# Two layers of a four-layer image network: the first layer's normalisation with pixels on the partitions, and the second layer's patch transform ahead of its input convolution

## The chip, the core and the metric

The kernel runs on one NeuronCore of a Trainium2 chip. The metric is the device time of one execution in microseconds (us), all data already in the chip's memory. PE is the matrix engine, PEld its weight loads, DVE the vector engine, ACT the scalar engine, POOL the engine that here issues gathers, SP the queue that issues the other transfers.

## The reference, cut to what matters

The input is 4 images of 48 channels of 256 x 256 pixels in f32. Four layers follow each other, each with a group normalisation ahead and a residual sum behind. The change touches the first two.

```
first layer:   qkv = depthwise3x3(conv1x1(x))            # q, k, v of 96 channels each
               out = irfft2(rfft2(q_patch) * rfft2(k_patch))   # 8 x 8 patches
               normed = (out - mean_c(out)) / sqrt(var_c(out) + 1e-5) * gamma + beta
               y = conv1x1(v * normed)
second layer:  y = w_in @ x                              # 48 -> 288 channels
               y = irfft2(rfft2(y_patch) * fft_mask)     # 8 x 8 patches, mask by channel
               y = depthwise3x3(y);  y = w_out @ (gelu(y1) * y2)
```

The mean and the variance of the first layer are over the 96 channels of one pixel. In the second layer `w_in` mixes channels and the patch transform mixes pixels, so that either may be done first. The third layer reads boxes of an integral image at computed places; the fourth is like the second.

## The kernel before, in words

`build` runs per image: first layer (`layer0`), second layer (`layer1`), integral image, front of the third layer. The boxes of the third layer are gathers (`Boxes`, POOL), their arithmetic is on DVE and their transposes on PE. They run inside other layers: image b's boxes, half of them, inside the first layer of image b + 1, the other half inside its second layer. So image 0 has both layers without boxes, and images 1 to 3 have them with boxes. The last image's boxes run inside the fourth layer.

Every engine has its own instruction list, written out by hand in program order; semaphores tie them together (`wait_ge`, `then_inc`). Nothing reorders the work.

**First layer.** A strip is 8 rows; an image has 32 strips, a strip has four steps of 512 pixels: 128 steps per image, 512 in all. `pipeline` (L407) unrolls eight steps in a loop body. In a step `n` PE does, in this order: the q and k convolutions of the first half (`conv_qk`, L516 and L519, pixels on the output's partitions); the output convolution of step n - 2 (L552); with boxes, at every other step, the transposes of one box unit (`boxes.turn`, L1803); for step n - 1 the inverse transform (L563, channels on the partitions); the second half of `conv_qk`; for step n - 1 the mean's removal as a product with a 96 x 96 matrix (L575), the v convolution (`conv_pass`, L285 and L289), and the variance (L584, one column per 128 pixels); the forward transforms of step n (L533); and for step n - 1 the spread of 1/sqrt over the channels' partitions (L592). ACT evacuates: `conv` L617, squares L628, root L631, `rb` L642, gamma and beta L645, copies of q and k L610 and of the spectra L638, and the split of the operands into two parts (L298). DVE has the reciprocal L707, the spectral products L714, the normalised value L719, its product with v L724, the residual sum L688 with statistics L692, the other half of the split L303, and with boxes the `blend` of one unit at odd steps (L1760 to L1777).

**Second layer.** A strip of 8 rows has 16 tiles of 128 pixels; 33 strips per image pass (`pipeline`, L804, two strips in a loop body). At slot t of a strip PE does the input convolution of tile t (L975, 49 rows deep, 304 columns), the forward transform of tile t - 1 (L918), the inverse of tile t - 2 (L925, three products of 128 columns), taps of the depthwise convolution of the strip before (L943, in small tiles of the array side by side), and at some slots the output convolution (L996 to L1002) and a box unit's transposes (L1803). ACT copies between the first two products (L1043), DVE multiplies by the mask (L1100) and does the rest of the depthwise convolution as a chain (L1111, L1114), the products with the gelu, the residual and, with boxes, the box arithmetic.

**Boxes.** POOL issues 16 gathers per unit. Each waits for a count (`paced`) that PE raises 16 times per unit, and may run ahead of it by `lead`. There are two buffers for gathered data (`used` frees one).

## Time and profile before

| what | us |
|---|---|
| median of the runs | 25524.35 |
| lowest and highest of 3 | 25506.17, 25534.23 |
| the profiled execution, and its span | 25507.03, 25505.5 |
| PE busy in the span | 23815.7 (93%) |
| DVE, POOL, ACT busy | 15811.9, 10957.5, 7039.7 |
| mean granted clock of PE | 0.951 |

Busy times of PE are ends as modelled of pipelined products, so a span that is full of them may still be spent on few columns. A slot of PE's time is better read from the start of one group to the start of the next. "PEclk" is the granted share of full clock; 1.00 is 2.4 GHz, a half is 1.2 GHz. In a window's row each number in brackets is a count of instructions.

### The profile page before, as it was taken

To read this page: it belongs to the slowest core of one execution; us is meant where nothing else is said; L and a number is where in the kernel's file an instruction comes from. 1 tells how busy PE (TensorE), PEld (TensorE's weight loads), DVE (VectorE), ACT (ScalarE), POOL (GpSimd) and SP (SyncE) were. 2 spreads that over 40 slices of the span, in tenths; PEclk is the share of its full clock that TensorE was granted. 3 is DMA by queue.
4 is the path that set the end of the run, shared out by engine and by line. 5 is a ranking of instruction groups with operands and counts; after the bars stand their busy time and mean duration, and the time that the engine had idled before them with its cause. 6 is when DMAs were issued, how large, how long until landed. Compare 5 with 4: busy or idle time off the path is not lost. (4 is left out here: it accounts for less than half of the span.)

```text
span 25505.5 us, 440196 instructions
## 1 busy us (share of the span) xinstructions
PE 23815.7 (93%) x147480; PEld 16191.6 (63%) x147480; DVE 15811.9 (62%) x23975; ACT 7039.7 (28%) x13096; POOL 10957.5 (43%) x8564
## 2 busy tenths in 40 slices
PE   6998998989999999899999988999999889998999
PEld 5775555667765556577655565777555647676767
DVE  4445555556668874566688845665888556666643
ACT  2333332123333321233333301333333112222222
POOL 0000000046656640366566602665666118787820
PEclk9999998899999998999999979999999799999999
DMA  3220001444432224444322234443222246666643
GB/s 81 57 62 26 20 21 43 115 100 102 99 76 80 79 69 110 105 102 100 80 80 78 75 94 111 101 102 84 79 79 80 82 116 136 136 142 133 140 92 73
DMA packets 875645, 2256.60 MB, mean 88 GB/s; under 512 B 257480, under 2 KB 509132, under 8 KB 762800
## 3 DMA queue, kind: packets, MB, share of 16 engines
q1 hardware_dynamic: 454512, 1309.67, 22.8%
q0 software_dynamic: 419840, 928.94, 14.4%
q8 instruction: 902, 14.78, 0.2%
q14 instruction: 391, 3.20, 0.0%
HBM read 1860.59 MB, written 385.13 MB: 88 GB/s over the span
## 5 line engine op out<-in xcount | busy, mean ns | idle before, releaser
L1706 POOL DMA_INDIRECT e_got<-table,e_idx x6144 | 7892.7, 1285 | 4230.8 <-issue 1766.9
L1722 POOL DMA_INDIRECT e_got<-table,e_idx x2048 | 2776.9, 1356 | 706.8 <-issue 492.6
L1114 DVE SCALAR_TENSOR_TENSOR b_acc<-b_z,b_dwc,b_acc 112x1024 f32<-112x1024 f32 x2112 | 2617.4, 1276 | 4.2
L285 PE MATMUL d_p<-d_xs,d_ws 125*96 125x512 f32 x9216 | 2480.7, 414 | 80.8 <-issue 57.2
L516 PE MATMUL a_p_qk<-a_wst,a_stack 125*128 125x192 f32 x12288 | 2424.1, 333 | 26.1 <-DMA a_stack<-in_xp 8.4
L1043 ACT ACTIVATE b_ys<-b_p_in 128x304 f32<-128x304 f32 x2112 | 893.8, 423 | 5223.8 <-PE b_p_in L975 5223.7
L943 PE MATMUL b_p_conv<-b_z,b_diag_a 64*64 64x512 f32 x19008 | 2277.7, 599 | 1.5 <-DVE b_g_a L1129 1.5
L1760 DVE TENSOR_TENSOR e_got<-e_got,e_wt 128x1536 f32<-128x1536 f32 x1024 | 1772.5, 1747 | 693.2 <-DMA e_got<-table,e_idx 690.2
L1100 DVE TENSOR_TENSOR b_ym<-b_p_f,b_mask 128x304 f32<-128x304 f32 x2112 | 1001.3, 474 | 1796.3 <-PE b_p_f L918 1785.8
L516 PEld LDWEIGHTS a_p_qk<-a_wst,a_stack 125*128 125x128 f32 x12288 | 2012.1, 190 | 123.8 <-ACT a_qh L638 80.2
L925 PEld LDWEIGHTS b_p_z<-const,b_ym 128*66 128x66 f32 (+2 forms) x12672 | 1649.3, 171 | 429.4 <-issue 32.9
L285 PEld LDWEIGHTS d_p<-d_xs,d_ws 125*96 125x96 f32 x9216 | 1479.5, 166 | 665.2 <-issue 84.8
L925 PE MATMUL b_p_z<-const,b_ym 128*66 128x128 f32 (+2 forms) x12672 | 1773.2, 276 | 13.0 <-ACT b_z L1031 12.8
L975 PE MATMUL b_p_in<-b_w,b_xt 66*128 66x304 f32 x4224 | 1632.2, 469 | 161.7 <-issue 157.4
L1233 POOL DMA_DIRECT2D i_x<-planes x128 | 66.3, 518 | 3796.9 <-issue 2339.0
L975 PEld LDWEIGHTS b_p_in<-b_w,b_xt 66*128 66x128 f32 x4224 | 674.2, 195 | 1502.8 <-issue 1489.6
L918 PE MATMUL b_p_f<-b_ys,const 128*128 128x304 f32 x4224 | 1466.5, 428 | 5.3 <-DVE b_ym L1100 5.3
L310 PE MATMUL c_p_g<-c_stack,c_wst 125*96 125x512 f32 x3072 | 1430.3, 602 | 26.0 <-issue 26.0
L1766 DVE TENSOR_TENSOR e_got<-e_got 128x1536 f32<-128x1536 f32 (+1 forms) x1024 | 1387.1, 1355 | 24.2
L285 PE MATMUL a_p_v<-a_xs,a_ws 125*96 125x512 f32 x4608 | 1371.4, 442 | 0.0
L707 DVE RECIPROCAL a_rs<-a_sd 128x4 f32<-128x4 f32 x512 | 89.6, 175 | 1962.3 <-ACT a_sd L631 1962.3
L943 PEld LDWEIGHTS b_p_conv<-b_z,b_diag_a 64*64 64x64 f32 x19008 | 625.8, 132 | 873.9 <-issue 750.9
(274 smaller groups left out, 40024.3 us busy)
## 6 DMA issues: line engine op xcount, KB each, us to landing
e_got<-table,e_idx POOLq DMA_INDIRECT x8192
a_stack<-in_xp SPq DMA_DIRECT2D x256, 387.0 KB
c_stack<-planes SPq DMA_DIRECT2D x256, 387.0 KB
d_stack<-planes SPq DMA_DIRECT2D x256, 387.0 KB
table<-i_acc SPq DMA_DIRECT2D x256, 384.0 KB, 2.3
b_x<-planes SPq DMA_DIRECT2D x132, 395.1 KB
b_xr<-planes SPq DMA_DIRECT2D x264, 197.5 KB
planes<-b_out SPq DMA_DIRECT2D x264, 197.5 KB
```

What stands on the lines that cost most here:

```text
L285: mm = pe.matmul(out, ws[i][:, dx, lo:hi], xs[j][:, r0:r0 + QROWS, dx:dx + W], start=(dx == i == j == 0), stop=False)
L310: pe.matmul(out, wst[:, dx, lo:hi], stack[:, r0:r0 + QROWS, dx:dx + W], start=(dx == 0), stop=False)
L516: m = pe.matmul(dst_, st[:, row, dx + 128 * t:dx + 128 * t + 128], wst[:, dx, 0:2 * C2], start=(dx == 0), stop=False)
L918: pe.matmul(p_f[:, 0:NC], env.c("dft"), ys[k % 2][:], start=True, stop=True).then_inc(f_ready, 1)
L925: mm = pe.matmul(p_z[g][0:MZ[g], k % 4 * 128:k % 4 * 128 + 128], ym[k % 2][:, LO[g]:LO[g] + MZ[g]], env.c("idft"), start=True, stop=True)
L943: mm = pe.matmul(p_conv[r][size * c:size * (c + 1), :], diag[size * r:size * (r + 1), k, :], zs[g][size * r:size * (r + 1), QROWS * q + dy ...
L975: pe.matmul(p_in[:, 0:NC], xt[par][:, t, :], w[:], start=True, stop=True).then_inc(in_ready, 1)
L1114: dve.scalar_tensor_tensor(out=a, in0=rows, scalar=dwc[0:M[D], D, k:k + 1], in1=a, op0=ALU.mult, op1=ALU.add).then_inc(chain, 1)
L1706: pool.indirect_dma_start(out=self.got[q][:, t, c * REC:(c + 1) * REC], out_offset=None, in_=self.flat, in_offset=bass.IndirectOffsetOnAxi ...
L1722: pool.indirect_dma_start(out=self.got[q][:, t, c * REC:(c + 1) * REC], out_offset=None, in_=self.flat, in_offset=bass.IndirectOffsetOnAxi ...
L1760: dve.tensor_tensor(part, part, self.wt[i][:, at:at + 32].unsqueeze(2).broadcast_to([128, 32, C]), ALU.mult).then_inc(self.halved, 1)
L1766: dve.tensor_tensor(got[:, :, 0:half], got[:, :, 0:half], got[:, :, half:2 * half], ALU.add).then_inc(self.halved, 1)
```

## The change

First layer: the inverse transform is done as two products with the transform as stationary operand, one per half of the pixels, into partitions 0 to 63 and 64 to 127 (`p_o`, 384 columns: 4 tiles of 96 channels). Pixels now lie on the partitions, so the sum over channels is along the row. ACT takes the sum and the sum of squares with an accumulating output (`accum_out`, four instructions each, one per 96 columns), the root, and the normalised value with a scale and a bias per pixel (four instructions); DVE adds `shift`. PE then transposes `nrm` back (four products with the identity, into `p_c`), and ACT applies gamma and beta (`gain`). The 96 x 96 product, the variance's four products and the spread of 1/sqrt are gone. The output convolution of step n - 2 stands behind the second half of `conv_qk`. On DVE the product with v opens the step, the spectral products close it, and a box unit's blend is spread over two steps. POOL's lead goes from 16 to 20.

Second layer: two neighbouring tiles of 49 input planes are taken together on 113 partitions (a second transfer loads the planes shifted by 16 pixels). PE turns them to pixels (`turned`, 128 columns), transforms them (`spectrum`, 128 columns), and then convolves each tile's spectrum to 304 columns (`widen`, two products from partitions 0 to 63 and 64 to 127, into two banks). ACT copies between them. The multiplication by the mask is done for two tiles at even slots, with four buffers instead of two.

The diff, cut to its core and moved left:

```diff
-        boxes.gather(pool, 0, U, 16)
+        boxes.gather(pool, 0, U, 20)
...
-        if back2:
-            pe.wait_ge(t3_ready, n - 1)
-            pe.wait_ge(sd_ready, n - 1)
-            pe.wait_ge(res_ready, n - 2)
-            pe.matmul(p_y[0:WIDE, :], wo[:], t3[k % 2][:], start=True, stop=True).then_inc(y_ready, 1)
...
-            pe.wait_ge(t1_ready, n - 1)
+            pe.wait_ge(gain_ready, n - 1)
             boxes.turn(pe, *turned(u, k), p_c)
...
-            pe.wait_ge(rb_ready, n - 1)
-            for t in range(4):
-                for h in range(2):
-                    m = pe.matmul(p_o[0:C2, t * 128 + h * 64:t * 128 + h * 64 + 64], prod[(k - 1) % 2][:, h, t, :],
-                                  env.c("combine"), start=True, stop=True)
-                    if beat and t == h == 0:
-                        boxes.beat(m)
+            pe.wait_ge(nrm_ready, n - 1)
+            for h in range(2):
+                m = pe.matmul(p_o[64 * h:64 * h + 64, 0:4 * C2], env.c("combine"),
+                              prod[(k - 1) % 2][:, h, :, :], start=True, stop=True)
+                if beat and h == 0:
+                    boxes.beat(m)
             m.then_inc(o_ready, 1)
         if front:
             conv_qk(k, n, 1)
+        if back2:
+            pe.wait_ge(t3_ready, n - 1)
+            pe.wait_ge(res_ready, n - 2)
+            pe.matmul(p_y[0:WIDE, :], wo[:], t3[k % 2][:], start=True, stop=True).then_inc(y_ready, 1)
         if back:
-            pe.wait_ge(o_copied, n)
-            pe.wait_ge(t1_ready, n - 1)
-            if boxes and turn_box:
-                boxes.bank_free(pe, *turned(u, k))
-            pe.matmul(p_c[0:C2, :], env.c("center"), conv[:], start=True, stop=True).then_inc(c_ready, 1)
...
             conv_pass(pe, p_v[0:C2, :], ws, we, xs[(k - 1) % 2], xe[(k - 1) % 2], 0, 0, C2,
                       boxes.beat if beat else None, (1, 8)).then_inc(v_ready, 1)
...
-            pe.wait_ge(sq_ready, n)
-            pe.wait_ge(res_ready, n - 1)
-            for t in range(4):
-                m = pe.matmul(p_y[:, t:t + 1], sq[:, 128 * t:128 * t + 128], env.c("mean96"), start=True, stop=True)
-            m.then_inc(var_ready, 1)
         if front:
             transforms(n, k)
...
-            pe.wait_ge(rs_ready, n)
+            pe.wait_ge(nrm_ready, n)
+            pe.wait_ge(gain_ready, n - 1)
+            if boxes and turn_box:
+                boxes.bank_free(pe, *turned(u, k))
             for t in range(4):
-                m = pe.matmul(p_o[0:C2, 128 * t:128 * t + 128], rs[:, t:t + 1].broadcast_to([128, C2]), env.c("ident"), start=True, stop=True)
+                m = pe.matmul(p_c[0:C2, 128 * t:128 * t + 128], nrm[:, t, :], env.c("ident"), start=True, stop=True)
...
+        if back2:
+            act.wait_ge(turned_ready, n - 1)
+            act.wait_ge(t3_ready, n - 2)
+            act.activation(gain[:], p_c[0:C2, :], ACT.Identity, bias=beta[:], scale=gamma[:]).then_inc(gain_ready, 1)
...
         if back:
             act.wait_ge(o_ready, n)
-            act.wait_ge(c_ready, n - 1)
-            act.activation(conv[:], p_o[0:C2, :], ACT.Copy).then_inc(o_copied, 1)
+            act.wait_ge(nrm_ready, n - 1)
+            for t in range(4):
+                s = act.activation(junk[:, t, :], p_o[:, C2 * t:C2 * t + C2], ACT.Copy, accum_out=total[:, t:t + 1])
+            s.then_inc(total_ready, 1)
+            act.wait_ge(total_ready, n)
+            act.wait_ge(shift_ready, n - 1)
+            act.activation(mu[:], total[:], ACT.Copy, scale=-1.0 / C2).then_inc(mu_ready, 1)
+            act.wait_ge(mu_ready, n)
+            for t in range(4):
+                s = act.activation(junk[:, t, :], p_o[:, C2 * t:C2 * t + C2], ACT.Square, bias=mu[:, t:t + 1],
+                                   accum_out=square[:, t:t + 1])
+            s.then_inc(sq_ready, 1)
         if front:
             copy_qk(1)
+        if back:
+            act.wait_ge(sq_ready, n)
+            act.wait_ge(rs_ready, n - 1)
+            act.activation(sd[:], square[:], ACT.Sqrt, bias=env.eps[:, 0:1], scale=1.0 / C2).then_inc(sd_ready, 1)
...
-            act.wait_ge(c_ready, n)
-            act.wait_ge(var_ready, n - 1)
-            act.activation(sq[:], p_c[0:C2, :], ACT.Square).then_inc(sq_ready, 1)
-            act.wait_ge(var_ready, n)
-            act.wait_ge(rs_ready, n - 1)
-            act.activation(sd[:], p_y[:, 0:4], ACT.Sqrt, bias=env.eps[:, 0:1]).then_inc(sd_ready, 1)
+            act.wait_ge(shift_ready, n)
+            act.wait_ge(turned_ready, n - 1)
+            for t in range(4):
+                s = act.activation(nrm[:, t, :], p_o[:, C2 * t:C2 * t + C2], ACT.Identity,
+                                   bias=shift[:, t:t + 1], scale=rs[:, t:t + 1])
+            s.then_inc(nrm_ready, 1)
...
-        if back:
-            act.wait_ge(b_ready, n)
-            act.wait_ge(t1_ready, n - 1)
-            act.activation(rb[:], p_o[0:C2, :], ACT.Copy).then_inc(rb_ready, 1)
-            act.wait_ge(t1_ready, n)
-            act.wait_ge(t3_ready, n - 1)
-            act.activation(t1[:], t1[:], ACT.Identity, bias=beta[:], scale=gamma[:]).then_inc(t2_ready, 1)
...
         if back2:
-            kk = (k - 2) % 8
-            r0 = QROWS * (kk % 4)
-            rows = out[kk // 4][:, r0:r0 + QROWS, 1:1 + W]
-            dve.wait_ge(y_ready, n - 1)
-            if kk % 4 == 0:
...
-            dve.scalar_tensor_tensor(out=rows, in0=p_y[0:CP, :].rearrange("p (y x) -> p y x", x=W), scalar=bo[:, 0:1],
-                                     in1=rows, op0=ALU.add, op1=ALU.add).then_inc(res_ready, 1)
...
-        if boxes and turn_box:
-            boxes.residual(dve, *turned(u, k), p_c)
+            dve.wait_ge(gain_ready, n - 1)
+            dve.wait_ge(v_ready, n - 1)
+            dve.wait_ge(y_ready, n - 3)
+            dve.tensor_tensor(t3[k % 2][:], p_v[0:C2, :], gain[:], ALU.mult).then_inc(t3_ready, 1)
...
-        if boxes and front and k % 2:
-            boxes.blend(dve, u, k // 4, k // 2 % 2)
+        if boxes and front:
+            for part in ((1, 2) if k % 2 else (0,)):
+                boxes.part(dve, u, k // 4, k // 2 % 2, part)
+        if boxes and turn_box:
+            boxes.residual(dve, *turned(u, k), p_c)
+        if back2:
+            kk = (k - 2) % 8
+            r0 = QROWS * (kk % 4)
+            rows = out[kk // 4][:, r0:r0 + QROWS, 1:1 + W]
+            dve.wait_ge(y_ready, n - 1)
+            if kk % 4 == 0:
...
+            dve.scalar_tensor_tensor(out=rows, in0=p_y[0:CP, :].rearrange("p (y x) -> p y x", x=W), scalar=bo[:, 0:1],
+                                     in1=rows, op0=ALU.add, op1=ALU.add).then_inc(res_ready, 1)
         if back:
             dve.wait_ge(sd_ready, n)
-            dve.wait_ge(b_ready, n - 1)
+            dve.wait_ge(nrm_ready, n - 1)
             dve.reciprocal(rs[:], sd[:]).then_inc(rs_ready, 1)
...
-            dve.wait_ge(y_ready, n - 2)
-            dve.tensor_tensor(t3[(k - 1) % 2][:], p_v[0:C2, :], t1[:], ALU.mult).then_inc(t3_ready, 1)
+            dve.wait_ge(rs_ready, n)
+            dve.tensor_tensor(shift[:], mu[:], rs[:], ALU.mult).then_inc(shift_ready, 1)
+        if back2:
+            dve.wait_ge(res_ready, n - 1)
+            q = n - n_first - 2
...
+            for h in range(2):
+                bank = p_f[1] if h == 0 else p_qk[1]
+                dve.wait_ge(qh_copied, 2 * n + h + 1)
...
+                dve.tensor_tensor(prod[k % 2][:, h, :, :].rearrange("p t c -> p (t c)"), bank[0:NPROD, 0:4 * C2],
+                                  qh[:, h, :, :].rearrange("p t c -> p (t c)"), ALU.mult).then_inc(prod_ready, 1)
...
-xt = [sb(f"xt{i}", [WIDE, NT, 128]) for i in range(2)]
-x, xr, out = sb("x", [CP, SROWS, WP]), sb("xr", [128, 2, QROWS, WP]), sb("out", [128, 2, QROWS, WP])
...
+xt = [sb(f"xt{i}", [128, NH, 128]) for i in range(2)]
+xp = [sb(f"xp{i}", [128, 128]) for i in range(2)]
+xf = [sb(f"xf{i}", [128, 128]) for i in range(2)]
...
-ym = [sb(f"ym{i}", [128, NC]) for i in range(2)]
+ym = [sb(f"ym{i}", [128, NC]) for i in range(4)]
...
-p_in, p_f, p_y = pb("p_in"), pb("p_f"), pb("p_y")
+p_in, p_y = [pb("p_in0"), pb("p_in1")], pb("p_y")
...
+        sp.dma_start(x[0:CP, :, :], planes(src, b, 0, CP, s * SROWS + 1, SROWS)).then_inc(x_loaded, 16)
+        sp.dma_start(x[64:PAIR, :, :], shifted(src, b, 0, CP, s * SROWS + 1, 16)).then_inc(x_loaded, 16)
...
+    def turned(n, i, k):
+        if k == 0:
+            pe.wait_ge(xt_ready, n + 1)
+        pe.wait_ge(masked, n * NT + 2 * (k - 1))
+        pe.wait_ge(t_copied, n * NH + k)
+        pe.matmul(p_in[0][:, FROM:FROM + 128], xt[i][:, k, :], env.c("ident"), start=True, stop=True).then_inc(t_ready, 1)
     def spectrum(n, k):
-        pe.wait_ge(in_copied, n * NT + (k + 1))
-        pe.wait_ge(masked, n * NT + k)
-        pe.matmul(p_f[:, 0:NC], env.c("dft"), ys[k % 2][:], start=True, stop=True).then_inc(f_ready, 1)
+        pe.wait_ge(t_copied, n * NH + (k + 1))
+        pe.wait_ge(masked, n * NT + 2 * k)
+        pe.wait_ge(f_copied, n * NH + k)
+        pe.matmul(p_in[1][:, FROM:FROM + 128], xp[k % 2][:], env.c("dft"), start=True, stop=True).then_inc(f_ready, 1)
+    def widen(n, k, more):
+        pe.wait_ge(t_copied, n * NH + (k + 2 if more or k + 2 < NH else NH))
+        pe.wait_ge(f_copied, n * NH + (k + 1))
+        pe.wait_ge(masked, n * NT + 2 * k)
+        for h in range(2):
+            pe.matmul(p_in[h][:, 0:NC], xf[k % 2][64 * h:64 * h + 64, :], w[64 * h:64 * h + 64, :],
+                      start=True, stop=True).then_inc(in_ready, 1)
...
-            if front:
-                if t == 0:
-                    pe.wait_ge(xt_ready, n + 1)
-                pe.wait_ge(in_copied, n * NT + t)
-                pe.matmul(p_in[:, 0:NC], xt[par][:, t, :], w[:], start=True, stop=True).then_inc(in_ready, 1)
-            if front and t >= 1:
-                spectrum(n, t - 1)
-            if mid and t == 0:
-                spectrum(m, NT - 1)
+            if front and t % 2 == 0:
+                widen(n, t // 2, more)
...
+            if front and t % 2:
+                if t + 3 < NT:
+                    turned(n, par, t // 2 + 2)
+                elif more:
+                    turned(n + 1, 1 - par, (t - 13) // 2)
+                if t + 1 < NT:
+                    spectrum(n, t // 2 + 1)
+                elif more:
+                    spectrum(n + 1, 0)
...
-        act.activation(xt[i][0:CP].rearrange("p t (y x) -> p t y x", x=16),
-                       x[:, :, 1:1 + W].rearrange("p y (t x) -> p t y x", x=16), ACT.Copy).then_inc(xt_ready, 1)
+        act.wait_ge(x_loaded, (n - 1) * 32)
+        act.wait_ge(t_ready, (n - 1) * NH)
+        act.activation(xt[i][0:PAIR].rearrange("p t (y x) -> p t y x", x=16),
+                       x[:, :, 1:1 + W].rearrange("p y (t g x) -> p t g y x", g=2, x=16)[:, :, 0], ACT.Copy).then_inc(xt_ready, 1)
+    def copy_turned(n, k):
+        act.wait_ge(t_ready, n * NH + (k + 1))
+        act.wait_ge(f_ready, n * NH + (k - 1))
+        act.activation(xp[k % 2][:], p_in[0][:, FROM:FROM + 128], ACT.Copy).then_inc(t_copied, 1)
+    def copy_spectrum(n, k):
+        act.wait_ge(f_ready, n * NH + (k + 1))
+        act.wait_ge(in_ready, n * NT + 2 * (k - 1))
+        act.activation(xf[k % 2][:], p_in[1][:, FROM:FROM + 128], ACT.Copy).then_inc(f_copied, 1)
...
-            if front:
-                act.wait_ge(in_ready, n * NT + (t + 1))
-                act.wait_ge(f_ready, n * NT + (t - 1))
-                act.activation(ys[t % 2][:], p_in[:, 0:NC], ACT.Copy).then_inc(in_copied, 1)
+            if front and t % 2:
+                if t + 3 < NT or more:
+                    copy_turned(n + (t + 3) // NT, (t // 2 + 2) % NH)
+                if t + 1 < NT or more:
+                    copy_spectrum(n + (t + 1) // NT, (t // 2 + 1) % NH)
...
     def weigh(n, k):
-        dve.wait_ge(f_ready, n * NT + (k + 1))
-        dve.wait_ge(inv_ready, n * NT + (k - 1))
-        dve.tensor_tensor(ym[k % 2][:], p_f[:, 0:NC], mask[:], ALU.mult).then_inc(masked, 1)
+        dve.wait_ge(in_ready, n * NT + (k + 1))
+        dve.wait_ge(inv_ready, n * NT + (k - 3))
+        dve.tensor_tensor(ym[k % 4][:], p_in[k % 2][:, 0:NC], mask[:], ALU.mult).then_inc(masked, 1)
...
-                weigh(n, t - 1)
-            if mid and t == 0:
-                weigh(m, NT - 1)
+            if front and t % 2 == 0:
+                weigh(n, t)
+                weigh(n, t + 1)
```

## Rows read from the trace of the kernel before

**Rows 1.** The page, part 1: busy us, share of the span, instructions.

```profile
PE 23815.7 (93%) x147480; PEld 16191.6 (63%) x147480; DVE 15811.9 (62%) x23975; ACT 7039.7 (28%) x13096; POOL 10957.5 (43%) x8564
```

**Rows 2.** Windows: stretch and length, busy us (instructions) by engine, PEclk, DMA, GB/s.

```profile
1003.49:1123.60 120.11, 119.00 (x704) 92.66 (x704) 55.58 (x97) 44.95 (x89) 0.00 (x0) 1.00 0.27 60
6009.76:6133.32 123.56, 122.41 (x736) 96.06 (x736) 75.40 (x109) 45.02 (x89) 80.33 (x65) 1.00 0.45 100
3082.50:3208.10 125.60, 123.22 (x928) 65.33 (x928) 73.46 (x98) 40.72 (x74) 0.00 (x0) 0.97 0.07 21
8139.20:8269.40 130.20, 125.79 (x961) 68.20 (x961) 107.39 (x134) 40.75 (x74) 85.00 (x64) 0.97 0.29 79
```

**Rows 3.** Timeline of PE, one step of the first layer: start, us, line, count.

```profile
1003.49 1.07 PE L552 MATMUL a_p_y<-a_t,a_wo 96*66 96x512 f32 x2
...
1004.40 1.50 PE L563 MATMUL a_p_o<-const,a_prod 94*96 94x64 f32 x16
...
1005.74 1.19 PE L516 MATMUL a_p_qk<-a_wst,a_stack 125*128 125x192 f32 x6
...
1008.40 1.02 PE L575 MATMUL a_p_c<-a_conv,const 96*96 96x512 f32 x2
...
1012.04 0.95 PE L584 MATMUL a_p_y<-const,a_sq 96*128 96x1 f32 x8
...
1012.93 0.56 PE L533 MATMUL a_p_f<-a_qk,const 64*94 64x384 f32 x1
...
1013.32 0.48 PE L533 MATMUL a_p_f<-a_qk,const 64*94 64x384 f32 x1
...
1013.65 0.48 PE L533 MATMUL a_p_f<-a_qk,const 64*94 64x384 f32 x1
...
1014.39 1.11 PE L592 MATMUL a_p_o<-const,a_rs 128*96 128x128 f32 x8
...
1015.48 1.24 PE L516 MATMUL a_p_qk<-a_wst,a_stack 125*128 125x192 f32 x6
...
1018.48 0.65 PE L552 MATMUL a_p_y<-a_t,a_wo 96*66 96x512 f32 x1
```

**Rows 4.** Groups by line and shape, second layer, two strips with boxes.

```profile
L1002 PE MATMUL b_p_y<-b_g_d,b_wo 112*64 112x512 f32 x16 | 4.3, 618 | 0.0
```

**Rows 5.** Groups by line and shape, whole span, ACT.

```profile
L645 ACT ACTIVATE a_t<-a_t,a_beta,a_gamma 96x512 f32<-96x512 f32 x512 | 416.0, 812 | 386.8 <-DVE a_t L719 386.8
...
L617 ACT ACTIVATE a_conv<-a_p_o 96x512 f32<-96x512 f32 x512 | 303.6, 593 | 1225.5 <-PE a_p_o L563 1225.5
...
L631 ACT ACTIVATE a_sd<-a_p_y,eps 128x4 f32<-128x4 f32 x512 | 134.7, 263 | 1248.8 <-PE a_p_y L584 1248.8
```

**Rows 6.** Timeline of DVE in the first layer with boxes.

```profile
6028.23 3.40 DVE L1760 TENSOR_TENSOR e_got<-e_got,e_wt 128x1536 f32<-128x1536 f32 x2
```

**Rows 7.** Timeline of PE in the second layer, around the head of the loop.

```profile
8130.03 0.68 PE L975 MATMUL b_p_in<-b_w,b_xt 66*128 66x304 f32 x2
...
8130.55 0.68 PE L918 MATMUL b_p_f<-b_ys,const 128*128 128x304 f32 x2
...
8131.06 0.82 PE L925 MATMUL b_p_z<-const,b_ym 128*66 128x128 f32 x6
...
8131.81 2.81 PE L943 MATMUL b_p_conv<-b_z,b_diag_e 32*32 32x512 f32 x48
...
8139.17 1.38 PE L975 MATMUL b_p_in<-b_w,b_xt 66*128 66x304 f32 x2 [4.56 <-issue]
...
8140.34 1.22 PE L918 MATMUL b_p_f<-b_ys,const 128*128 128x304 f32 x2
```

**Rows 8.** Groups of POOL, eight steps of the first layer with boxes.

```profile
L1706 POOL DMA_INDIRECT e_got<-table,e_idx x65 | 82.3, 1266 | 43.6 <-issue 15.0 <-PE a_p_qk L519 11.2 <-PE a_p_f L533 7.3
```

**Rows 9.** Windows again: the integral image after the second layer, and the fourth layer.

```profile
4300.00:4640.00 340.00, 300.87 (x1764) 297.25 (x1763) 156.26 (x562) 28.43 (x58) 14.34 (x28) 0.68 0.32 101
21500.00:23900.00 2400.00, 2197.86 (x11623) 1665.60 (x11624) 1496.74 (x2024) 530.01 (x930) 1926.00 (x1419) 0.96 0.66 138
```

108 lines of the change are left out of this document (55 added, 53 removed).

## The prediction

> **What bounds the kernel now.** I read the page's busy times first [rows 1]: PE is busy 93% of the span, DVE 62%, POOL 43%, ACT 28%. An average over layers says little, so I then took windows of whole periods [rows 2]: eight steps of the first layer without and with boxes (120.11 and 123.56 us), and two strips of the second layer from loop head to loop head, without and with boxes (125.60 and 130.20 us). The reader is to see that PE is busy for all but 1 us in the first layer's two windows and that no other engine comes near; in the second layer PE is idle for 2.4 and 4.4 us, and DVE, with boxes, has 107.39 of 130.20 us filled. So both layers go at PE's pace now, and DVE is the next limit in the second layer with boxes. Last I read PE's timeline by starts [rows 3, 7]: what a group costs is the time from its start to the next group's.
>
> **First layer, the slots of one step** [rows 3]: output convolution 0.91 us (1003.49 to 1004.40), inverse transform 1.34, second half of q and k 2.66, mean and v convolution together 3.64, variance 0.89, forward transforms 1.46, spread of 1/sqrt 1.09, first half of q and k with the wait behind it 3.00. Sum 14.99.
>
> Removed: the variance, 0.89. The mean's product, two passes of 512 columns as the output convolution has: 0.91 less about 0.03 for the change of shape, 0.88. The wait of 0.13 (my reading of 3.00 less 2.66, the rest being the change of shape) at the output convolution goes too: PE waits there for `t3`, and the output convolution now stands 3.4 us later, behind the inverse transform and the second half of q and k. Where the step then waits next is weighed below.
>
> Changed: the inverse transform has 16 passes of 64 columns and gets four of 384 columns, two by two in the array's two column halves. That form is in the trace in the second layer's output convolution [rows 4]: 16 passes of 512 columns keep PE busy for 4.3 us, 1.08 per four, though two passes of 512 one after the other cost 0.88. So the halves run side by side. The forward transforms show two passes of 384 columns per 0.33 us (1013.32 to 1013.65) [rows 3], so I take 2 x 0.33 + 0.09 for the switch = 0.75. Bounds: 0.65, and 1.40 if the halves run one after the other. Gain taken 0.59. The spread's eight passes of 128 columns become eight passes of 128 columns of transposes: no change.
>
> Sum: 0.89 + 0.88 + 0.13 + 0.59 = 2.49 us per step, a step of 12.50. The trace has 128 steps without boxes and 384 with; with boxes the turn of a unit adds (123.56 - 120.11)/4 = 0.86 every second step, unchanged, so 15.44 becomes 12.95. Gains: 128 x 2.49 = 319 us and 384 x 2.49 = 956 us.
>
> What could stand in PE's way is the chain from the inverse transform to the transposes: ACT's four sums, the negated mean, four squares, a copy of q and k, the root, two splits; DVE's reciprocal and shift; ACT's four normalisations. Between the two PE has 2.66 + 0.91 + 2.76 + 1.46 = 7.8 us of other work. The prices: an ACT operation over 512 columns takes 593 ns with no pointer, 812 with scale and bias as pointers, one over 4 columns with one pointer 263 [rows 5]. By the slope from 4 to 512 columns I estimate 96 columns at 0.26 us, 0.34 with a bias, 0.44 with both. No row shows an accumulating output: between nothing and a whole further small operation, 0.26, each. I take 0.1, since the four sums read no more than the one copy (L617) that they replace. Then the squares end 4 x 0.26 + 0.2 + 4 x 0.34 + 0.8 = 3.4 us after the inverse transform, the root at about 4.2, the splits at 5.3; DVE's reciprocal stands behind the residual sum, which waits for the output convolution (3.6 us, plus 0.3 of latency, plus 0.74), so at about 4.9, shift 5.2; the normalisations end at 7.0. That is 0.8 us inside the cover. With the accumulation at 0.26 they end at 7.6 to 7.8: still just inside. ACT's total rises from 45 us per eight steps [rows 2] to some 65 of 100.
>
> DVE with boxes: 75.40 us per eight steps [rows 2], less one product of 0.6 and plus a shift of 0.2 per step, some 72 of 103.6. The two weighings of a unit take 3.40 us [rows 6] and now stand ahead of the residual sum at even steps. From the end of `t3` (1 us before the inverse transform ends, at most) they end 2.4 us behind it, the box residual 1.4 later, at 3.8, and the sum is due at 3.9. This is tight but covered, if the gathers have landed.
>
> Gathers: 16 per two steps. At present each takes 1.27 us of POOL plus 0.30 of issue [rows 8], 25 us per unit; two steps will last 25.9. So POOL goes from half idle to nearly full and a late gather will hold DVE, hence PE, now and then. The unit is also weighed a step earlier, and the lead of four more makes good half a step of that. Between nothing and the fourth layer's rate (1419 gathers in 2400 us, 1.69 each, 27.0 per unit [rows 9], 0.55 per step over mine, 211 us) I take 50 us. The second layer's extra transfer falls where the DMA share is 0.07 to 0.29 [rows 2]; I price it at nothing.
>
> **Second layer, two tiles** [rows 7]: convolution 0.52 and transform 0.51 each, 2.06 for two tiles; the inverse 0.75 for six passes of 128 columns stays. Added: four passes of 128 columns at 0.125, 0.50; and the widened pair, four passes of 304 columns from two row halves. The first layer's forward transforms are such pairs and run side by side [rows 3], so 2 x 0.25 + 0.05 = 0.55. Bounds 0.50 and 1.05. Gain 2.06 - 1.05 = 1.01 per two tiles, 8.1 per strip. Without boxes DVE has 73.46 us of work in 125.60 [rows 2] and stays under PE's: 33 strips x 8.1 = 267 us.
>
> With boxes DVE is the limit. Its 107.39 us of busy time per two strips and about 0.04 us for each of its 134 instructions (my estimate of the pauses between dependent ones) give 112.8. PE would need 123.6 - 16.2 = 107.4 between the loop's heads. The head costs more: PE idles 4.56 us at it and then runs its first products at half clock, 1.17 us against 0.52 [rows 7], some 6.8 us in all on top of 2 x 61.6. PE can't be far ahead of DVE there: `turned` at odd slots waits for both mask products of the slot before, on DVE. I take the head's 6.8 us as added to DVE's time, 119.6 per two strips against 130.20; the bounds are 113 (hidden wholly) and 123. Gain 5.3 per strip, 99 strips: 525 us; 500 with the first strips of each image, which have no full load.
>
> Starts of the four images cost some 10 us (a serial chain turned, copied, transformed, copied; a memset ahead of the first load).
>
> **Sum**: 319 + 956 - 50 + 267 + 500 - 10 = 1982 us off the profiled execution's 25,507, so 23,525. That execution lay 17 us under the median of three; the median of the changed kernel I put at 23,540.
>
> **Rivals.**
> 1. POOL sets the pace of the first layer with boxes, at the fourth layer's rate: 161 us more, 23,700. For it: 25 of 25.9 us is nearly no slack, and gathers of over 4 us hide in that mean of 1.27. Against it: the fourth layer's DMA share is 0.66, this one's would be 0.54.
> 2. The second layer's loop head is hidden under DVE's backlog: 113 per two strips, 8.6 per strip, 850 in place of 500 less the load of the first strips, 23,250. Against it stands the wait of `turned`.
> 3. ACT's small operations are late: an accumulation at 0.5 us each puts eight of them 3.2 us behind my 0.8 and beyond the cover by some 2.4 us; 512 steps x 2.4 = 1230, 24,770; half of that, 24,150, at 0.35. For it: no row has such an instruction.
> 4. The halves don't run side by side in these new forms: 0.65 x 512 = 333, and 0.5 x 8 x 33 = 132, and about 130 in the strips with boxes: 24,135. Against it are rows 3 and 4.
> 5. The other side: in the second layer with boxes PE waits for DVE at every odd slot, and the clock falls as at the loop head and stays at half. At present it falls after a gap of 4.56 us [rows 7], and where PE's work is broken by waits for long, the window's mean is 0.68 [rows 9]. PE's 53.5 us per strip would be about 105, 40 over today's 65.1, x 99 = 3960; with the gains of the first layer and of image 0 (1482) the time is 27,985. It decides once some 37% of these strips' time is at half. Against it: the waits that I see are about 1 us, between stretches of taps, and the first layer has such short waits at a clock of 1.00 [rows 2].
>
> On this rival the Trainium skill, page "TensorE: Matmul & The Clock Gate", section "HAM oscillation — how this bites in real kernels", says that a loop in which each burst of matmuls is followed by a wait pays the return to the half rate on every turn. By that rule, and only if my 1 us were long enough, the kernel would be the slower one; the loop head in rows 7 does just what the rule says, and no row shows it for waits of 1 us.
>
> **How the numbers follow.** Forecast 47%, rival 1 17%, rival 2 12%, rival 3 14%, rival 4 6%, rival 5 4%. The range of 80% reaches from 23,200 (below rival 2) to 24,250 (over rivals 1 and 4 and the half of rival 3). A measurement of this kernel tells 0.2%, about 50 us, from no change. Only rival 5 or a far worse rival 3 ends slower: faster 0.95, same 0.01, slower 0.04.
>
> **What would show it.** Eight steps of the first layer should take 100 us without boxes and 103.6 with; the inverse transform's slot 0.75; PE's wait ahead of the transposes under 0.2 us. In the second layer two strips take 109 us without boxes and 120 with, where DVE's idle time is at the loop head only. I am wrong if ACT's accumulating operations take over 0.5 us, if PE waits for `nrm` or for `f_copied` in every step, or if the granted clock in the second layer with boxes is under 0.9.

## The result, and the profile after

The changed kernel takes 23,558.65 us (median of 4; 23,545.67 to 23,576.81), against 25,515.26 for the kernel before: ratio 0.9233, interval 0.9217 to 0.9249. The forecast was 23,540. Its profiled execution has a span of 23,544.1 us at a mean granted clock of 0.945.

The page of the changed kernel, part 1, against [rows 1]:

```profile
PE 21720.1 (92%) x136216; PEld 14130.0 (60%) x136216; DVE 15356.9 (65%) x23979; ACT 7710.4 (33%) x22312; POOL 10986.6 (47%) x8568
```

TensorE (PE) lost 2,096 us of work and stays the engine that is busy all the time. ScalarE (ACT) has only 671 us more work, but 9,216 more instructions.

Windows of the changed kernel, with the columns of [rows 2]: eight steps of the first layer without and with boxes, then two strips of the second without and with boxes.

```profile
1134.64:1239.23 104.59, 102.33 (x530) 73.17 (x528) 51.26 (x98) 63.24 (x236) 0.00 (x0) 0.98 0.31 70
5223.66:5334.42 110.76, 105.70 (x562) 77.40 (x561) 70.41 (x108) 62.91 (x234) 88.57 (x66) 0.98 0.52 113
3036.63:3146.55 109.92, 107.31 (x928) 52.72 (x929) 71.98 (x98) 33.64 (x74) 0.00 (x0) 0.97 0.10 31
7748.69:7862.77 114.08, 110.34 (x961) 55.45 (x961) 105.08 (x134) 33.67 (x74) 78.41 (x64) 0.98 0.36 98
```

The forecast for the four was 100, 103.6, 109 and 120. The first two are longer, and PE is now idle for 2.3 and 5.1 us in them where it was idle for 1 us before; the third is close to the forecast (109.0 in the mean of image 0's loop turns), the fourth 6 us shorter.

PE's timeline of one undisturbed step of the first layer, which answers to [rows 3]:

```profile
1058.94 1.02 PE L568 MATMUL a_p_y<-a_t,a_wo 96*66 96x512 f32 x2
1059.40 2.66 PE L285 MATMUL a_p_v<-a_xs,a_ws 125*96 125x512 f32 x9
...
1062.69 0.56 PE L534 MATMUL a_p_f<-a_qk,const 64*94 64x384 f32 x1
...
1064.16 1.11 PE L583 MATMUL a_p_c<-const,a_nrm 128*96 128x128 f32 x8
1065.25 1.24 PE L517 MATMUL a_p_qk<-a_wst,a_stack 125*128 125x192 f32 x6
...
1068.05 0.87 PE L557 MATMUL a_p_o<-a_prod,const 94*64 94x384 f32 x4
1068.85 1.24 PE L517 MATMUL a_p_qk<-a_wst,a_stack 125*128 125x192 f32 x6
...
1071.56 0.59 PE L568 MATMUL a_p_y<-a_t,a_wo 96*66 96x512 f32 x1
```

From start to start it is 12.62 us: output and v convolution 3.75, forward transforms 1.47, transposes 1.09, q and k with the combine pass between them 2.80 + 0.80 + 2.71. The combine slot (L557) tells that the column halves run side by side: 0.80 us for four passes of 384 columns.

PE around the second layer's loop head, against [rows 7]:

```profile
7742.83 2.81 PE L971 MATMUL b_p_conv<-b_z,b_diag_e 32*32 32x512 f32 x48
7748.69 0.94 PE L945 MATMUL b_p_in<-b_w,b_xf 64*128 64x304 f32 x4 [3.05 <-issue]
7749.56 1.55 PE L953 MATMUL b_p_z<-const,b_ym 128*66 128x128 f32 x6
```

Where the 1,961 us between the two spans lie, by stretches of the two traces (the first layer from its first to its last q/k product, the second from there to the integral image):

| stretch | forecast gain | measured |
|---|---|---|
| first layer, image 0 | 319 | 257 (1,918 to 1,661) |
| first layer, images 1 to 3 | 906 | 745 (1,989 to 1,741 each) |
| second layer, image 0 | 267 | 258 |
| second layer, images 1 to 3 | 500 | 718 |
| starts; fourth layer, whose code is the same | -10; 0 | within the rows above; -21 (4,535 to 4,557) |

The total is right by luck: the first layer gives 223 us less than forecast and the second 209 us more. What the experiments had to find is each of these errors. Some 43 us of the second layer's two rows are the passage to it, from the last q/k product to its own first product, which is 9 to 12 us shorter in each image (80 to 70 in image 0, about 71 to 60 in the others). Experiment 1 shows that most of this comes with the first layer's change.

ACT's groups of the changed kernel over the whole span, which take the place of [rows 5]:

```profile
L639 ACT ACTIVATE a_nrm<-a_p_o,a_shift,a_rs 128x96 f32<-128x96 f32 x2048 | 715.1, 430 | 268.1 <-DVE a_shift L716 263.9 <-issue 4.2
L620 ACT ACTIVATE a_junk<-a_p_o,a_mu 128x96 f32<-128x96 f32 x2048 | 669.4, 339 | 16.6
...
L613 ACT ACTIVATE a_junk<-a_p_o 128x96 f32<-128x96 f32 x2048 | 482.5, 250 | 426.7 <-PE a_p_o L557 426.7
L613 ACT ACTIVATION_READ_ACCUMULATOR a_junk<-a_p_o 128x1 f32 x2048 | 423.5, 207 | 0.0
```

An accumulating output is an instruction of its own, 0.207 us long, though the next one starts 0.09 us after it (1148.47 and 1148.56 us in one step). The estimates of 0.26, 0.34 and 0.44 us for 96 columns hold: 0.25, 0.34, 0.43.

Two kinds of stall are new. In image 0, PE's waits (engine, line, what it waited for; us, times, longest):

```profile
PE a_p_f L534 <- ACT a_qk L601: 27.7, 13, 2.9
PE a_p_c L583 <- ACT a_nrm L639: 5.8, 8, 0.9
```

Thirteen times, once for each turn of the loop. ACT's own waits there name nothing on which it depends:

```profile
ACT a_qk L601 <- issue: 53.5, 13, 4.5
ACT a_gain L606 <- issue: 50.4, 13, 4.8
```

ACT stands still for about 3.9 us at the jump back (before L606) and 4.1 in the middle of the body (before L601), while everything it needs is ready. In images 1 and 2 there are no such gaps, and image 3 has the 13 at the jump alone. The trace also records the jump instruction itself (L408): from it to the next instruction that ACT's sequencer takes up there are 4.4 us in image 0 and 4.6 in image 3 (medians), and 0.24 in images 1 and 2, which run the same code. So the sequencer itself stands still there.

In image 1 (4850 to 6450 us) PE waits for something else:

```profile
PE a_p_c L583 <- ACT a_nrm L639: 37.2, 21, 5.0
```

and VectorE's (DVE) timeline at one of these times says why:

```profile
5228.30 1.76 DVE L1803 TENSOR_TENSOR e_got<-e_got,e_wt 128x1536 f32<-128x1536 f32 x1 [8.44 <-DMA e_got<-table,e_idx]
...
5232.08 0.16 DVE L714 RECIPROCAL a_rs<-a_sd 128x4 f32<-128x4 f32 x1
5232.27 0.16 DVE L716 TENSOR_TENSOR a_shift<-a_mu,a_rs 128x4 f32<-128x4 f32 x1
```

The weights wait 8.44 us for gathered records; reciprocal and shift stand behind them in DVE's order, `nrm` behind shift, and PE's transposes behind `nrm`, 4.99 us. From 5216 to 5231 the DMA engines are busy without a break (1.04), with SyncE's loads of the next strip (`a_stack`, `a_rest`, `a_out`, the box unit's weights) among the gathers. And the wait costs more than itself. Three windows:

```profile
5216.00:5231.00 15.00, 12.93 (x71) 9.32 (x69) 5.91 (x7) 6.04 (x25) 11.83 (x11) 1.00 1.04 178
5229.00:5233.00 4.00, 0.00 (x0) 0.00 (x0) 3.80 (x7) 0.53 (x2) 3.39 (x3) 1.00 0.95 230
5233.90:5238.00 4.10, 4.08 (x19) 4.08 (x20) 2.51 (x5) 1.48 (x3) 2.16 (x2) 0.62 0.31 87
```

After 5 us without work PE runs at a granted clock of 0.62 over 4.1 us, that is for most of it at 1.2 GHz in place of 2.4. This step takes 18.90 us, 6.28 over the ordinary.

### The profile page after: what moved, and what is told of

Read it like the earlier page. It is cut to its first block and busy times, and to the rows that moved or that the text cites. A ratio compares the mean times of both kernels' runs of the same rounds, so it can differ in the third digit from the quotient of the medians.

```text
span 23544.1 us, 427591 instructions
## 1 busy us (share of the span) xinstructions
PE 21720.1 (92%) x136216; PEld 14130.0 (60%) x136216; DVE 15356.9 (65%) x23979; ACT 7710.4 (33%) x22312; POOL 10986.6 (47%) x8568
## 5 line engine op out<-in xcount | busy, mean ns | idle before, releaser
L1803 DVE TENSOR_TENSOR e_got<-e_got,e_wt 128x1536 f32<-128x1536 f32 x1024 | 1781.8, 1751 | 1038.5 <-DMA e_got<-table,e_idx 1035.5
L953 PEld LDWEIGHTS b_p_z<-const,b_ym 128*66 128x66 f32 (+2 forms) x12672 | 1513.9, 172 | 1104.6 <-issue 888.1
L953 PE MATMUL b_p_z<-const,b_ym 128*66 128x128 f32 (+2 forms) x12672 | 1860.0, 286 | 15.3 <-ACT b_z L1070 15.3
L1056 ACT ACTIVATE b_xp<-b_p_in 128x128 f32<-128x128 f32 x1056 | 292.7, 277 | 4699.9 <-PE b_p_in L932 4689.7
L1144 DVE TENSOR_TENSOR b_ym<-b_p_in,b_mask 128x304 f32<-128x304 f32 x2112 | 899.5, 468 | 779.4 <-PE b_p_in L945 775.1
L971 PE MATMUL b_p_conv<-b_z,b_diag_e 32*32 32x512 f32 x19008 | 1118.8, 596 | 2.1 <-DVE b_g_a L1172 2.1
L285 PEld LDWEIGHTS a_p_v<-a_xs,a_ws 125*96 125x96 f32 x4608 | 747.9, 162 | 540.2 <-issue 284.9
L709 DVE SCALAR_TENSOR_TENSOR a_out<-a_p_y,a_bo,a_out 49x512 f32<-49x512 f32 x512 | 379.5, 741 | 1038.7 <-PE a_p_y L568 1038.2
L520 PE MATMUL a_p_qk<-a_wrs,a_rest 66*128 66x192 f32 x4096 | 1010.9, 327 | 0.0
```

The lines of the kernel that those rows point to most:

```text
L285: mm = pe.matmul(out, ws[i][:, dx, lo:hi], xs[j][:, r0:r0 + QROWS, dx:dx + W], start=(dx == i == j == 0), stop=False)
L520: m = pe.matmul(dst_, rt[:, row, 128 * t:128 * t + 128], wrs[:, 0:2 * C2], start=False, stop=True)
L953: mm = pe.matmul(p_z[g][0:MZ[g], k % 4 * 128:k % 4 * 128 + 128], ym[k % 4][:, LO[g]:LO[g] + MZ[g]], env.c("idft"), start=True, stop=True)
L971: mm = pe.matmul(p_conv[r][size * c:size * (c + 1), :], diag[size * r:size * (r + 1), k, :], zs[g][size * r:size * (r + 1), QROWS * q + dy ...
L1144: dve.tensor_tensor(ym[k % 4][:], p_in[k % 2][:, 0:NC], mask[:], ALU.mult).then_inc(masked, 1)
L1803: dve.tensor_tensor(part, part, self.wt[i][:, at:at + 32].unsqueeze(2).broadcast_to([128, 32, C]), ALU.mult).then_inc(self.halved, 1)
```

## The experiments

Twelve kernels. "The changed kernel" is 23,558.65 us throughout. Totals of kernels timed on different chips can differ by some 10 to 20 us, and the integral image's stretch, the same code in all, goes from 360 to 417 us between traces; so the stretches of the traces are compared, not the totals alone.

**1. Each layer's change alone.** The old function `layer1` beside the new `layer0`, and the other way round.

```
first_only:   layer0 of after, layer1 of before
second_only:  layer0 of before, layer1 of after
```

> The first layer as changed, the second as it was before. The terms of the forecast ask for 319 us in image 0 and 906 us in images 1 to 3: 25,515 - 1,225 = 24,290 us. Theory from the two traces: the first layer's stretch in the changed kernel became shorter by 257 us in image 0 and by 745 us in images 1 to 3, and nothing of the second layer's gain depends on it, so 25,515 - 1,001 = 24,515 us (24,480 to 24,550). Rival: part of the changed kernel's gain exists only with both layers changed (the transfers and gathers of one run under the other), and the time is over 24,560 us.

> The first layer as before, the second as changed. The terms of the forecast ask for 267 + 500 - 10 = 757 us: 24,758 us. Theory from the two traces: the second layer's stretch became shorter by 258 us in image 0 and by 718 us in images 1 to 3: 25,515 - 976 = 24,540 us (24,500 to 24,580). If the two sum to the whole change, this ratio and the other's gains add up to 1,957 us. Rival: the second layer's gain beyond the forecast came with the changed first layer, and alone it gives 757 us.

Measured: 24,546.7 us, ratio 0.9616 (0.9600 to 0.9632), as expected, and 24,605.2 us, 0.9639 (0.9623 to 0.9655), 25 us beyond the range. In the traces the new first layer gives 248, 251, 243 and 221 us in images 0 to 3, as against 257, 246, 250 and 249 with both changed. The new second layer gives 244, 232, 233 and 222 us within its own products (from the first that turns or convolves a tile to the last inverse), as against 250, 225, 227 and 236 with both changed. The shorter passage between the two layers, 43 us over the four images, comes with the first layer's change (44 us with it alone, 9 with the second alone). The expectation for `second_only` had counted it with the second layer, which is most of what it missed. So each layer keeps its own gain, and the error of the forecast is in each layer, not in how they meet.

The single gains add up to 977 + 919 = 1,896 of 1,957 us. Of the missing 61, 21 are the fourth layer's, whose time is 4,557 and 4,562 us here, as with the whole change: either change costs them, so the sum of the two counts them twice. Another 38 are the first layers, which gain less when alone: ScalarE's gaps are then in images 0, 1 and 3, not in 0 and 3, and image 3, with 26 gaps, is 27 us longer than with both.

**2. ScalarE without the sums** (mean and variance are left out; ones stand in for them).

```
-  s = act.activation(junk[:, t, :], p_o[...], ACT.Copy, accum_out=total[:, t:t + 1])
+  s = act.activation(junk[:, t, :], p_o[...], ACT.Copy)
   (the squares likewise; DVE fills total and square with ones once)
```

> The changed kernel without the accumulated outputs of the first layer's copies and squares (the sums that give mean and variance are left out; two tiles filled with ones stand in for them). That takes 8 instructions of 0.20 us a step out of ScalarE's list. Theory A (ScalarE's list is too long to be fetched in time: gaps of 3 to 5 us at the loop's head and in the body's middle, which hold the whole step): the gaps go, one step in eight of image 0 falls from 15 to 18.7 us to 12.6, which gives about 27.7 + 5.8 us per 320 us, some 130 us over image 0 and 27 us or more in image 3; sum 100 to 200 us faster, 23,360 to 23,460 us. Rival B (the gaps come from something else in the loop, say its own branch and address arithmetic, or transfers): they stay, and the time moves by less than 30 us. Rival C: ScalarE's busy time itself is what holds PE: then every step, not one in eight, becomes shorter.

Measured: 23,503.85 us, 0.9213 (0.9198 to 0.9229). The gaps are gone in all images (26 and 13 before, now 0), and image 0's first layer is 1,617 us in place of 1,661. A step without a stall stays at 12.61: rival C is out. The mechanism of theory A is there, and my size for it was wrong by three: the 27.7 + 5.8 us were those of the whole image, which I had taken for those of 320 us. Image 3, which was to gain 27 us or more, gains nothing: its first layer takes 1,745 us, 1,740 before, though its 13 gaps are gone; experiment 3 shows what takes their place. Eight instructions less a step cure the gaps, but this changes length and place at once.

**3. Only the place.** 48 increments of a semaphore ahead of ScalarE's list in each image.

```
   act.wait_ge(weights_loaded, 16 * NLOAD * (b + 1))
+  for _ in range(48):
+      act.sem_inc(turn, 1)
```

> The changed kernel with 48 semaphore increments (a few tens of ns each) ahead of ScalarE's list in the first layer of every image: the loop's body is the same and as long, and only its place in the list moves, by 48, 96, 144 and 192 instructions in images 0 to 3. Theory P (each of the 13 gaps of an image is a fetch whose moment is set by where the body lies in the list): the images and places with gaps change (now image 0 at the jump back and in the middle, image 3 at the jump back, images 1 and 2 none), and the time moves by 10 to 60 us either way. Rival Q (the gaps depend on the body's length and on what else runs in that image, the others' loads in image 0 or the four gather buffers in image 3): the same images show the same 26, 0, 0 and 13 gaps, and the time is the same within 15 us.

Measured: 23,537.57 us, 0.9218 (0.9204 to 0.9232). The total tells little, the trace more: neither of the two gaps in any image (ScalarE's jump takes 0.24 us in all four), and eight steps of image 0 take 100.98 us, with PE busy for all but 0.07:

```profile
1112.13:1213.11 100.98, 100.91 (x531) 72.34 (x529) 50.59 (x96) 63.16 (x234) 0.00 (x0) 1.00 0.32 72
```

Image 0's first layer is 1,619 us, as without the sums. The body is the same, as long as before, and next to the same loads: rival Q falls. The best reading of the 3.9 us is then a wait for instructions whose moment depends on where the body lies. The traces show no engine waiting for instructions by name; "issue" at the same two places, thirteen times, that goes when the list is moved, is how far they reach.

What a gap costs is another matter. Image 3's first layer stays as long without its gaps, 1,746 us for 1,740. PE's waits there, changed kernel and this one:

```profile
PE a_p_c L1846 <- ACT a_gain L606: 27.1, 13, 2.3
```

```profile
PE a_p_c L583 <- ACT a_nrm L641: 41.7, 19, 5.9
```

The second kind of stall, that of the late gathers, comes up where the first has gone. So the gaps by themselves are worth 42 to 44 us in image 0 and nothing in image 3.

**4. Shorter list by other means.** The same mean and variance by another formula: one square over 384 columns on ScalarE; two sums, the square of the total and the variance on DVE.

```
-  4 copies and 4 squares with accum_out, mu
+  act.activation(junk, p_o[:, 0:4 * C2], ACT.Square)
+  dve.reduce_sum(total[:], p_o as (t c), axis=X);  dve.reduce_sum(square[:], junk[:], axis=X)
+  both = total * total;  var = square * -96 + both
```

> The changed kernel with the same result by a shorter list for ScalarE: one square over all 384 columns in place of 4 squares, 4 copies, their 8 accumulator reads and the mean, and on VectorE two sums over 96 channels for the 4 columns, the square of the total and the variance (E[x2] - mean2). ScalarE issues 16 instructions less a step, VectorE 4 more, about 1.4 us a step, where it is idle 4.6 us a step in images 1 to 3. Theory (the 3.9 us gaps after the jump back and in the body come from the length of ScalarE's list): image 0's first layer falls from 1,661 to about 1,617 us, as without the sums, image 3's by 10 to 30 us; 23,470 to 23,520 us if VectorE's additions stay hidden. Rival: the sums come after the box unit's part on VectorE, so shift and normalised pixels are late in the steps with boxes; at 0.5 us a step over 384 steps that is +190 us, 23,650 to 23,750 us.

Measured: 23,526.21 us, 0.9220 (0.9207 to 0.9233). Image 0's first layer 1,618 us, image 3's 1,725 (1,740 before), no gaps. DVE's sums take 0.55 us each and are hidden; the rival falls. The total misses the theory's range by 6 us.

DVE's own jump bears the reading out at a place where it costs nothing that shows. In the second layer, from DVE's jump (L810) to its sequencer's next instruction, the changed kernel has 4.0 us in image 1, 4.6 in image 2 and 0.3 in images 0 and 3; with this experiment's longer list for DVE ahead of it, it has 0.3 in all four.

**5. Gathers earlier.**

```
-  boxes.gather(pool, 0, U, 20)
+  boxes.gather(pool, 0, U, 28)
```

> The changed kernel with gathers of the first layer allowed 28 beats ahead of TensorE in place of 20 (12 gathers ahead of their unit rather than 4). Theory (GpSimd is the near bound there: it issues 16 gathers in 25.5 to 26 us of the 26.1 us that two steps take, waits for TensorE's beats only 45 us in 1,680, and the late gathers lie behind bursts of SyncE's loads that take 99% of the DMA engines for 10 us): a longer lead finds no time to use; within 20 us of the changed kernel, 23,540 to 23,580 us. Rival: the lead was what kept the gathers late; VectorE's 124 us of waits for them in image 1 halve, and the time falls by 50 to 80 us to about 23,490 us.

Measured: 23,547.63 us, 0.9230 (0.9216 to 0.9244): no difference. In image 1 DVE's waits for gathers go from 117.8 to 102.2 us and PE's for `nrm` from 37.2 to 31.1. GpSimd (POOL) has little time to make use of a longer lead: it is idle for 1,600 - 1,309 us, and 275 of these are its own issue. Part of its work is made longer by DVE: most gathers take 0.95 us, but 36 of the 1,024 of image 1 in the changed kernel (34 here) take over 4 us, up to 4.48, and all of these lie under the two weighings (L1803) and the box residual behind them.

**6. The taker later.** The box unit's parts behind reciprocal and shift.

```
   t3; others' statistics
-  box unit's part
   box residual; residual sum; reciprocal; shift
+  box unit's part
   statistics; lower halves; products
```

> The changed kernel with VectorE's box unit parts (the work on the gathered records) behind the residual sum, reciprocal and shift of its step rather than ahead of them. Theory (TensorE's 39.9 and 37.3 us of waits for the normalised pixels in images 1 and 2 come from gathers that land late and hold VectorE ahead of reciprocal and shift): those waits go, and what is late behind the parts, the product for the next step's combine pass, has its slack; 30 to 80 us faster, 23,480 to 23,530 us. Rival: 3.5 us of weights ahead of the product leave it no slack in every step with boxes: TensorE waits 1 to 2 us for it in each of 384 steps, 23,800 to 24,300 us.

Measured: 23,411.3 us, 0.9172 (0.9158 to 0.9186), 147 us under the changed kernel and beyond my range on the good side. Images 1 to 3 gain 49, 48 and 45, their first layers now at 1,691 to 1,695 us. Waits of DVE for gathers in image 1, changed kernel and this one:

```profile
L1803 DVE TENSOR_TENSOR e_got<-e_got,e_wt 128x1536 f32<-128x1536 f32 x120 | 206.9, 1748 | 117.8 <-DMA e_got<-table,e_idx 117.8
```

```profile
L1803 DVE TENSOR_TENSOR e_got<-e_got,e_wt 128x1536 f32<-128x1536 f32 x124 | 212.2, 1753 | 1.1
5215.18:5319.60 104.42, 104.35 (x562) 75.95 (x560) 69.26 (x108) 63.05 (x234) 76.83 (x65) 1.00 0.55 119
```

POOL's gathers in the same stretch, changed kernel and this one:

```profile
L1749 POOL DMA_INDIRECT e_got<-table,e_idx x954 | 1295.6, 1358 | 306.4 <-issue 261.8 <-PE a_p_qk L520 20.0 <-PE a_p_v L285 19.1
```

```profile
L1749 POOL DMA_INDIRECT e_got<-table,e_idx x973 | 1164.5, 1197 | 419.5 <-issue 235.3 <-DVE e_box L1817 128.5 <-PE a_p_qk L517 23.6
```

So the order does up to three things. What is late no longer stands ahead of shift, which I had expected. Nothing is late any more, which I had not. For that there are two candidates that this run doesn't separate. The records are wanted 7.7 us later in the step: the weighing starts 2.2 us behind the start of the output convolution (5217.33, 5215.18), and started 5.5 ahead of it (5218.12, 5223.66). And a gather now takes 1.20 us in the mean, not 1.36, none over 2.6: POOL, which had 1,557 of 1,600 us filled with gathers and their issue, has 1,400, and waits 128 us for DVE to free a buffer, so it is ahead. With the waits the half clock goes as well (1.00 over the eight steps), which is why 49 us come back in image 1 and not 37. In image 3 ScalarE's 13 gaps are still there, shorter (25 us in all for 53), and PE waits 0.2 us for them.

**7. Both remedies.**

> Both remedies together: the box unit's parts behind reciprocal and shift, and 48 increments ahead of ScalarE's list. The first took 147 us from the changed kernel in its own comparison, all of it in the first layers of images 1 to 3 (1,741 to 1,693 us each); the second took the 26 gaps of image 0 (1,661 to 1,619 us). They touch different images. Theory: they add up, 23,411 - 42 = 23,370 us (23,345 to 23,390). Rival: the gaps come back at another place, since every list after it moves again; then 23,400 to 23,440 us.

Measured: 23,362.81 us (5 runs), 0.9160 (0.9147 to 0.9172): faster than both kernels, 196 us under the changed one, 0.8%. First layers 1,617, 1,692, 1,694 and 1,694 us, no gap of ScalarE in any. The two remedies add up as expected.

> The box unit's parts behind reciprocal and shift, together with the short list for ScalarE (sums on VectorE) in place of the 48 increments. Theory: image 0's first layer 1,617 us as with the short list alone, images 1 to 3 1,690 us as with the parts late: 23,360 to 23,400 us, the same as with the increments. Rival: VectorE's four more instructions, now ahead of everything else of the step, and the late parts together leave the product too late: steps with boxes longer by 0.3 to 1 us, 23,450 to 23,750 us.

Measured: 23,389.05 us, 0.9166 (0.9152 to 0.9180); 1,617, 1,692, 1,693 and 1,694 us. Its interval overlaps that of the version with the increments, its first layers are the same within 1 us, and it needs no idle instructions. The rival falls: late parts and the sums leave the products in time.

**8. The unit whole again**, at every second step, in the late place.

```
-  for part in ((1, 2) if k % 2 else (0,)): boxes.part(dve, u, k // 4, k // 2 % 2, part)
+  if k % 2: boxes.blend(dve, u, k // 4, k // 2 % 2)
```

> The order with the box unit behind reciprocal and shift, and in addition the unit whole again in every second step, as before the change, in place of weights in the one step and halving and finish in the other. It is 7.8 us of VectorE work in one step. Theory (the product for the next step's combine pass is last on VectorE, and needs its slack): the odd step gets longer by some 2 to 4 us, 4 x 48 pairs and more of them, 23,700 to 24,100 us. Rival: VectorE, busy 66% of the time, catches up within the two steps and splitting the unit was of no use: 23,390 to 23,430 us, as with the split one.

Measured: 24,047.08 us, 0.9425 (0.9410 to 0.9439), first layers of images 1 to 3 at 1,903 to 1,907 us: 3.3 us per pair of steps over the split unit. The split is worth 636 us in this order. PE's waits in image 1:

```profile
PE a_p_o L557 <- DVE a_prod L731: 88.2, 54, 1.6
PE a_p_c L1845 <- DVE e_val L1819: 29.0, 54, 0.7
```

They make 2.2 us per pair. The rest goes with the clock, 0.96 over image 1 in place of 1.00. At one of these steps PE waits 0.55 and then 1.58 us, and then:

```profile
4840.00:4846.00 6.00, 3.87 (x25) 2.76 (x24) 5.86 (x12) 0.87 (x5) 4.63 (x5) 1.00 0.36 93
4846.00:4850.00 4.00, 4.00 (x16) 3.98 (x15) 0.54 (x1) 2.27 (x15) 2.93 (x4) 0.57 1.02 144
4850.00:4854.00 4.00, 4.00 (x17) 2.20 (x17) 2.81 (x6) 3.12 (x8) 3.08 (x4) 1.00 1.03 165
```

At 5794.50, after waits of 0.40 and 1.64 us, it stays at 1.00. The length of the waits doesn't decide it: of two steps with waits of 0.38 and 1.64 us, that at 5664.7 takes 15.9 us and that at 5187.7 takes 17.5. In image 1 the steps with such waits take 15.9 to 16.1, 17.5 to 17.8 or 19.0 us. What decides between them stays open.

**9. Is the second layer bound by DVE?** Six of 18 links of its chain cut to one row of pixels in images 1 to 3 (parts of three taps are left out).

```
   rows = zs[D][...]; a = acc[:, h, :]...
+  if boxes and k >= 6: rows, a = rows[:, 0:1, :], a[:, 0:1, :]
```

> The changed kernel with 6 of the 18 links of VectorE's chain cut to one row of 256 pixels in the second layer of images 1 to 3 (two thirds of three taps of one part of the depthwise convolution are left out). VectorE is relieved of about 6 us per strip of 57. Theory (with its box units the second layer is now bound by TensorE, not by VectorE as I had reckoned): almost nothing, under 0.5 us per strip, under 50 us in all. Rival (VectorE still sets the strip's length): 3 to 6 us for each of 99 strips, 300 to 600 us faster, 22,950 to 23,250 us.

Measured: 23,570.26 us, 0.9234 (0.9218 to 0.9249): no gain. The same 1,100 us of the second layer, changed kernel first:

```profile
6900.00:8000.00 1100.00, 1066.09 (x9210) 537.86 (x9206) 1008.52 (x1288) 323.11 (x709) 749.41 (x615) 0.98 0.36 97
```

```profile
6900.00:8000.00 1100.00, 1061.78 (x9180) 536.08 (x9176) 914.87 (x1282) 322.54 (x709) 701.50 (x613) 0.98 0.36 97
```

DVE has 94 us less to do, and PE gets through as many products (within 0.4%). In the means of images 1 to 3 two strips take 114.0 to 114.4 us in the changed kernel and 113.7 to 115.0 here. DVE doesn't set the length of a strip.

**10. The loop head of the second layer.** The 48 increments ahead of PE's list.

```
   pe.wait_ge(diag_ready, 36 * (b + 1))
+  for _ in range(48):
+      pe.sem_inc(turn, 1)
```

> The changed kernel with 48 increments ahead of TensorE's list in the second layer of every image. TensorE's jump back there takes 3.7 us and leaves a gap of about 3.1 us in each pair of strips, in all four images alike, so some 60 times, 190 us in all. Theory (as on ScalarE, a gap appears or not by the place of the body): in some images the jump gets short, and each such image's second layer is 40 to 50 us shorter. Rival (TensorE's body of two strips is longer than what can be kept or fetched ahead wherever it lies): the same 3 us at every jump, and the time within 15 us of the changed kernel's 23,558.

Measured: 23,614.35 us, 0.9257 (0.9243 to 0.9271), 56 us slower. PE's gap at the jump is 2.1 to 3.8 us, in all four images, where it was 2.1 to 3.6: as the rival has it. But the rival is not right on the time, for two reasons. The passage from the first layer to the second, where the increments stand, is 6 to 7 us longer in each image, 28 in all: the 48 increments take 7.25 us there (1926.98 to 1934.23 in image 0). And in image 3 alone a second gap has come 3 us behind the first, and the layer's own products take 1,872 us in place of 1,844:

```profile
16590.47 0.85 PE L947 MATMUL b_p_in<-b_w,b_xf 64*128 64x304 f32 x4 [2.52 <-issue]
16593.51 1.54 PE L955 MATMUL b_p_z<-const,b_ym 128*66 128x128 f32 x6 [2.19 <-issue]
```

So place matters on PE too, for the gap in the body, and for the one at the jump it doesn't. Why PE's jump always costs some 3 us in this loop and 0.3 in the first layer's stays open. One difference is the length: from jump to jump the trace has 1,986 to 2,059 instructions of PE in the second layer and 1,109 to 1,178 in the first. ScalarE has 323 in the changed first layer, 178 before, 259 without the sums and 187 in experiment 4, and of these four only the 323 show gaps, and not in every image. No run here varied the length alone.

## Why the prediction was right, and where it was wrong

**The mechanism, right; the total, luck on top.** The measured time is 19 us from the forecast because two terms of some 200 us were wrong in opposite directions. What removes the time was foreseen. The variance, the mean's product and the wait ahead of the output convolution are gone, the combine pass and the widened pair run side by side, and ScalarE's chain stays inside its cover. A step of 12.50 was forecast, 12.61 measured (the median of image 0): 0.05 in the combine slot (0.80 for 0.75), 0.08 in output and v convolution together. With boxes 13.05 for 12.95 (experiment 6, where nothing stalls). These 0.1 us make some 50 us over 512 steps.

**First layer, stalls, mis-sized: 223 us short.** 50 are the step above. 44 are ScalarE's gaps in image 0 (1,661 to 1,617 or 1,619 in experiments 2 and 3), for which the forecast had no term: it added up ScalarE's durations, found them inside the cover, which they are, and never asked what 18 more instructions a step do to the list. 143 in images 1 to 3 came back with the taker later (experiment 6), against 50 put down for late gathers; in image 3 of the changed kernel the waits are mostly behind ScalarE's gaps (27 us), but experiment 3 shows late gathers behind them. The remaining 36 are the starts: in the mended kernel of experiment 7 each of the images 1 to 3 begins 10 us later than before and image 0 begins 7 later (first layer less 128 steps). In image 1 DVE's longest wait for the first gathers is 25.0 us (12.7 before) and PE waits 25.5 us for a product of DVE behind it (18.4 before); the 7 us of image 0, which has no gathers, are not explained. That the unit is weighed a step earlier was in the text, half of it priced as made good by four more gathers of lead; experiment 5 shows that eight further ones do nothing for the time, so lead did not make it good.

**Second layer with boxes: the step that failed is "With boxes DVE is the limit".** I had 107.39 of work and 5.4 of pauses and added the loop head's 6.8. Measured are 114.08 per two strips. The pauses are not there: in the changed kernel DVE is busy for 105.08 of 114.08 and has idle time left, and a DVE that has 4.8 us less to do per strip changes nothing (experiment 9). The limit is PE: the text's own figure for it, 107.4 plus the head's 6.8, is 114.2. Rows 2 could have told it. DVE's 107.39 of 130.20 was filled to 82%; to take it for a limit at 113 I had to set a pause behind every instruction, and no row of idle time stood behind that 0.04. The gap at the head is 3.05 us here, 4.56 before, and it isn't hidden.

**The same layer without boxes**: 258 for 267 with 9 us of shorter passage in it, two strips 109.0 in the mean for 109.4. Here too two terms were off and cancel. The widened pair takes 0.71 us from start to start (median of 1,052), not 0.55, and the convolution slot that it replaces took 0.62 (median of 2,104), not the 0.52 of the one slot in rows 7.

**Sums that don't come out.** The chain on ScalarE ends at 7.0 with 0.1 us per accumulation; with 0.26, eight of them add 1.3 us, which is 8.3 and half a microsecond past the cover of 7.8, not "7.6 to 7.8: still just inside". The text's own rival 3 counts it so. It did no harm, as an accumulation costs 0.09. Rival 2 by its own terms is about 23,215, not 23,250. Rival 5's 37% takes the other strips at today's 65.1 us; at the forecast's 59.8 it is 45%.

**The rivals.** 1 (POOL sets the pace) is false as put: eight steps take 104.42 us once the order is mended, not 108. In the changed kernel's own order it came near, with 1,557 of 1,600 us filled. 2 (the head hidden) is false, the head's gap is in every pair. 3 (accumulations at 0.35 or 0.5) is false, 0.09 each by starts. 4 (halves in turn) is false: 0.80 us in the first layer's slot, against 1.40; in the second layer's pair 0.71, nearer to 0.50 than to 1.05. 5, the fall of the clock from short waits, did not happen in the second layer (0.98 with boxes). The Trainium skill, page "TensorE: Matmul & The Clock Gate", section "HAM oscillation — how this bites in real kernels", holds that a burst followed by a wait pays the slow rate at each turn. The step behind the wait of 5.0 us in image 1, at 0.62, agrees with it. What I had set against it, that waits of about 1 us don't do so, is not safe: experiment 8 shows the clock at 0.57 behind waits of 0.55 and 1.58 us, though not at every turn.

**The fourth layer's 21 us.** Its code is the same and it goes from 4,535 us to values between 4,539 and 4,562 in the thirteen changed traces, with no clear order by the lists ahead of it: experiment 5's kernel, whose lists are as long as the changed kernel's, has 4,545 us against 4,557. So more than half of the 21 us can come from one trace to the next, and the cause stays open.

## What to carry to other kernels

Where an engine has room in its busy time, count its instructions as well: a list that has grown can stop for 3 to 5 us at a jump or in the body, in some instances of the same loop and not in others, and a few idle instructions ahead of it show in one run whether it is that. Then look what the gap hides: where late gathers stood behind it, taking it away gave nothing. Put work that takes from a DMA behind, not ahead of, what the bounding engine waits for: here the order on an engine with a third of its time free was worth 48 us per image, and a longer lead nothing. And before calling an engine the next limit, look for its idle time in the rows; a pause per instruction that no row shows is not a term.

## What was not expected of the hardware

- An accumulating output on ScalarE is a second instruction: 0.207 us busy, 0.09 us by starts, 4,096 of them.
- Gaps of 3.4 to 4.8 us on ScalarE at the jump back and in the body, that 48 increments (or 8 instructions less a step) take away; on PE one of some 2 us that 48 increments bring, in one image of four.
- From a jump to the next instruction that ScalarE takes up 4.4 us or 0.24 for the same code in different images; the same on DVE, 4.0 to 4.6 us or 0.3.
- A gather of 0.95 us takes up to 4.48 where DVE's two weighings run beside it.
- PE at 0.62 of its clock for 4 us behind a wait of 5 us, and at 0.57 behind waits of 0.55 and 1.58 us, but at 1.00 behind 0.40 and 1.64; of two steps with waits of 0.38 and 1.64 us one takes 15.9 us and the other 17.5.
